# A transformer block on one core: fetches issued by ScalarE, row turns kept in order, masks ahead of the last additions, and three projections and splits moved

## The reference

```
h   = layernorm(x)                          # rows of 512
kqv = h @ Wqkv + bqkv                       # 16 heads of 32
s   = k q^T / sqrt(32); s = triu(s) - 10000 * tril(1, -1)
a   = softmax(s, axis=2) ; out = einsum('bnkq,bknh->bqnh', a, v)
x   = x + layernorm(out @ Wo + bo)
g,u = layernorm(x) @ Wg^T, layernorm(x) @ Wu^T   # Wg, Wu: 2048 x 512, (int - 128) * scale
x   = x + layernorm((silu(g) * u) @ Wd^T)   # the inner layernorm is of the new x
```

## Time and profile before

| What | Value |
|---|---|
| median of 3 runs | 1640.79 us (1640.74 to 1642.38) |
| profiled execution | 1639.89 us, of which span 1638.1 us |
| mean granted TensorE clock | 0.981 |
| TensorE busy | 1544.6 us, 94% of the span |
| VectorE, ScalarE, GpSimd busy | 57%, 49%, 36% |
| start, 0 to 78 us | TensorE busy 51.21 us, granted clock 0.91 |
| attention, 78 to 953 us | TensorE busy 816.92 us, granted clock 0.97 |
| feed-forward, 953 to 1638 us | TensorE busy 676.49 us, granted clock 1.00 |

### The profile page before, as it was taken

The page is one execution under the profiler, slowest core; times in us unless marked ns, Lnnn a source line. Parts: engine busy times, 40 slices in busy tenths (PEclk is TensorE's granted clock), DMA queues, the critical chain, the costliest instruction groups (busy, mean ns, idle before and its releaser), DMA issues.

```text
span 1638.1 us, 24488 instructions
## 1 busy us (share of the span) xinstructions
PE 1544.6 (94%) x9322; PEld 641.2 (39%) x9324; DVE 939.4 (57%) x1864; ACT 795.9 (49%) x1284; POOL 592.7 (36%) x809
## 2 busy tenths in 40 slices
PE   4899999998999999999977999999999999999997
PEld 2333334333333333333322244444444444444443
DVE  5666755788756887667756333564434343434344
ACT  5356676667666776667755633232222222222222
POOL 4335664677556766755755310020000000000001
PEclk8999999999999999999988999999999999999999
DMA  4212322224411233223345431221111111111000
GB/s 181 92 50 52 77 55 53 67 64 117 105 48 35 81 106 88 61 52 95 106 137 164 108 97 45 59 97 38 47 26 52 26 52 26 52 26 52 1 26 26
DMA packets 113398, 112.26 MB, mean 69 GB/s; under 512 B 69632, under 2 KB 69632, under 8 KB 113024
## 3 DMA queue, kind: packets, MB, share of 16 engines
q1 hardware_dynamic: 113280, 110.69, 23.7%
HBM read 45.37 MB, written 25.17 MB: 43 GB/s over the span
## 4 chain that ended last, share of the span: by engine, by line
PE 72%; DVE 10%; POOL 6%; ACT 4%; issue 4%; SPq 3%; DMA 1%; POOLq 0%; ACTq 0%; DVEq 0%
PE ps L976 25%; PE ps L897 16%; PE ps L993 12%; PE ps L960 10%; PE ps L934 5%; DVE mcol L1255 4%; SPq L753 3%; POOL pt L1467 2%; PE ps L910 2%; ACT pt L1109 1%; POOL rs L1387 1%; PE ps L918 1%; DVE st L1150 1%; DVE xh L650 1%; POOL pt L1458 1%
## 5 line engine op out<-in xcount | busy, mean ns | idle before, releaser
L1109 ACT ACTIVATE pt<-ps,nrm 128x512 f32<-128x512 f32 (+1 forms) x640 | 361.5, 647 | 222.0 <-PE ps L934 208.8
L976 PE MATMUL ps<-x2in,gu 128*128 128x512 f16 x2048 | 462.4, 379 | 0.1
L1255 DVE TENSOR_REDUCE mcol<-ps 128x1 f32<-128x512 f32 (+2 forms) x636 | 318.0, 566 | 139.3 <-PE ps L918 93.1
L976 PEld LDWEIGHTS ps<-x2in,gu 128*128 128x128 f16 x2048 | 200.2, 98 | 242.0 <-ACT sg L1130 0.6
L1384 POOL TENSOR_SCALAR rs<-mv 128x1 f32<-128x1 f32 x120 | 27.2, 226 | 652.4 <-DVE mv L1154 646.1
L1326 DVE SCALAR_TENSOR_TENSOR hf<-ps,usc,sg 128x512 f32<-128x512 f32 x128 | 96.1, 751 | 259.1 <-PE ps L976 245.6
L1135 ACT ACTIVATE hh<-hf 128x512 f16<-128x512 f32 x128 | 80.7, 631 | 258.8 <-DVE hf L1326 245.2
L1467 POOL TENSOR_TENSOR pt<-pt 128x1024 f32<-128x1024 f32 x84 | 201.5, 2421 | 1.8 <-ACT pt L1109 1.8
L934 PE MATMUL ps<-qpack,kpack 98*128 98x512 f16 (+3 forms) x768 | 163.6, 331 | 29.0 <-DVE mcol L1255 25.7
L993 PE MATMUL ps<-wd,hh 128*128 128x512 f16 x496 | 188.0, 379 | 0.0
L993 PE MATMUL ps<-wd,hl 128*128 128x512 f16 x496 | 188.0, 379 | 0.0
(11 more groups left out here) (125 smaller groups left out, 1592.8 us busy)
## 6 DMA issues: line engine op xcount, KB each, us to landing
qpack<-stage SPq DMA_DIRECT2D x192, 64.0 KB, 2.0
kpack<-stage SPq DMA_DIRECT2D x192, 64.0 KB, 2.0
xr<-in_x SPq DMA_DIRECT2D x32, 256.0 KB, 2.9
x1d<-xr SPq DMA_DIRECT2D x32, 256.0 KB, 2.3
x2d<-xh SPq DMA_DIRECT2D x32, 256.0 KB, 2.3
x1in<-x1d SPq DMA_DIRECT2D x8, 1024.0 KB, 5.8
out_x<-yy SPq DMA_DIRECT2D x32, 256.0 KB, 2.0
xin<-in_x SPq DMA_DIRECT2D x24, 256.0 KB, 2.9
```

The costliest lines, as they stand in the source:

```text
L976: mm = pe.matmul(bk, GU[:, c, m, i * 128:(i + 1) * 128], x2in[:, 1 - k, p, c, :], start=p == 0 and c == 0, stop=p == 1 and c == 3)
L1109: act.activation(Pt[:, PBUF[step], h, off:512], ps[:, BANK[job], off:512], ACT.Exp, scale=esc).then_inc(s_ex, 1)
L1255: mm = dve.tensor_reduce(mcol[:, n % 2, col:col + 1], scores, AX.X, ALU.max)
```

## The change

1. **Fetches by ScalarE.** A new job `act_fetch(i)` for i = 1 to 7 stands at the start of the step after the one that converts i - 1, and ScalarE issues the DMA. SP keeps fetches 0 and 8 to 23.
2. **Rows in order.** `row_work` keeps the normalised blocks in a list, and only the oldest of them may be turned. In steps 5 to 7 of the groups n % 4 == 1 nothing is turned.
3. **Projections.** In groups n % 4 == 2 the q and k projections stand at steps 3, 5, 7, 9 (before: 1, 3, 7, 9) and the v projections at 1, 2, 4, 6, 8 (before: 0, 2, 4, 6, 8). `qk(2, 0, 0)` leaves step (0, 1) and stands ahead of the groups, behind the last v projection and ahead of `packs(1)`.
4. **Sums.** In step 7 both additions stand behind the scores and masks (before: one ahead, one behind). The `den` of the summed blocks moves from step 9 to step 0 of the next group.
5. **Devs.** In steps 0 to 2 only the first `dev` stands ahead of the products; the others follow the scores.
6. **Halves of the result.** In groups 14 and 15 `halve` follows the scores.
7. **Split of Wo.** `split_o` 0 to 3 stand at (0, 3), (0, 4), (2, 3), (2, 4) (before: (0, 3) to (0, 6)).

```diff
--- before.py
+++ after.py
@@ -106,14 +106,15 @@
     b, g = divmod(n, 4)
     out = {}
     if n + 2 < NG:
-        for i, s in enumerate(((0, 2, 3, 7) if b else (1, 3, 7, 9), (0, 1, 2, 3), (1, 3, 7, 9), (1, 2, 3, 8))[g]):
-            out[s] = ("qk", n + 2, i % 2, i // 2)
+        for i, s in enumerate(((0, 2, 3, 7) if b else (None, 3, 7, 9), (0, 1, 2, 3), (3, 5, 7, 9), (1, 2, 3, 8))[g]):
+            if s is not None:
+                out[s] = ("qk", n + 2, i % 2, i // 2)
     if n == 0:
         for i, s in enumerate((0, 2, 5, 8)):
             out[s] = ("vproj", 4 + i)
     if b + 1 < B:
         first = 8 * b + 8 + (0, 0, 2, 7)[g]
-        for i, s in enumerate(((), (7, 9), (0, 2, 4, 6, 8), (0,))[g]):
+        for i, s in enumerate(((), (7, 9), (1, 2, 4, 6, 8), (0,))[g]):
             out[s] = ("vproj", first + i)
     if g == 3:
         for i, s in enumerate((5, 7, 9)):
@@ -147,7 +148,7 @@
         if g == 1 and b + 1 < B:
             chains += [(NS * n + (0, 1, 2, 3, 4, 5, 6, 7)[k], LN1, 8 * b + 8 + k) for k in range(8)]
     at = {}
-    untaken = 0
+    untaken = []
 
     def free(kind, step):
 
@@ -163,14 +164,19 @@
             kind = kinds[0]
             if kind == "residual" and ("wo_stats", t - 2) in at and at.get(("turn2", t - 2), step) >= step:
                 continue
-            if kind == "residual" and adding(step):
+            if adding(step) and (kind == "residual" or step // NS % 4 == 1 and kind in ("ln1_turn", "turn2")):
                 continue
             if kind == "ln1_stats" and t >= 10 and at.get(("ln1_norm", t - 2), step) + 2 > step:
                 continue
-            if kind in ("ln1_norm", "norm2") and untaken == 2 or kind in cost and not free(kind, step) and (
-                    room.get(step, 99) < cost[kind]):
+            if kind in ("ln1_norm", "norm2") and len(untaken) == 2 or (
+                    kind in ("ln1_turn", "turn2") and untaken[0] != t):
                 continue
-            untaken += {"ln1_norm": 1, "norm2": 1, "ln1_turn": -1, "turn2": -1}.get(kind, 0)
+            if kind in cost and not free(kind, step) and room.get(step, 99) < cost[kind]:
+                continue
+            if kind in ("ln1_norm", "norm2"):
+                untaken.append(t)
+            if kind in ("ln1_turn", "turn2"):
+                untaken.pop(0)
             if kind in cost and step in room and not free(kind, step):
                 room[step] -= cost[kind]
             at[kind, t] = step
@@ -186,13 +192,18 @@
     summed = step[0] < SUMS and step[1] == 1 and step[2] < 4
     out = [] if summed else [("den",) + step]
     out.append(("num",) + step)
-    if summed and step[2] > 0:
-        out += [("sum",) + step + (h,) for h in (0, 2) if h == 0 or s != 7]
-    return out + [("den", n, 1, 0)] * (s == NS - 1 and n < SUMS)
+    if summed and step[2] in (1, 2):
+        out += [("sum",) + step + (h,) for h in (0, 2)]
+    return [("den",) + step[:2] + (0,)] * (s == 0 and step[0] < SUMS) + out
 
 
 
 LAST = (124, 125, 126, 127)
+
+
+
+SPLIT_O = [(0, 3), (0, 4), (2, 3), (2, 4)]
+
 
 
 def order_of_jobs():
@@ -222,7 +233,7 @@
         if i == 6:
             plan += [("inverses", 3), ("vo_scale",)]
         add(("mjob", 0, i))
-    plan += [("mjoin", 0), ("mturn", 0)] + fill
+    plan += [("mjoin", 0), ("mturn", 0)] + fill + [("qk", 2, 0, 0)]
     plan += [("packs", 1), ("load_x", 8), ("load_x", 9)] + [("mjob", 1, i) for i in range(EARLY)]
 
     rows = {}
@@ -241,21 +252,27 @@
         for s, (j, kb) in enumerate(STEPS):
             here = rows.get(NS * n + s, [])
             add(("step", n, s))
-            plan += [("dev", DEV_FOR[job[0]], job[1]) for job in here if job[0] in DEV_FOR]
+            plan += [("act_fetch", i) for i in range(1, 8) if ffn_step(i - 1) + 1 == NS * n + s]
+            devs = [("dev", DEV_FOR[job[0]], job[1]) for job in here if job[0] in DEV_FOR]
+            soon = 1 if s < 3 else len(devs)
+            plan += devs[:soon]
             lot, of = (s + EARLY, n + 1) if s < NS - EARLY else (s + EARLY - NS, n + 2)
             if of < NG:
                 add(("mjob", of, lot))
             plan += [job for job in here if job[0] in ("ln1_turn", "turn2")]
-            if (s == 1 and n > 0) or s == 4:
-                add(("halve", n if s == 4 else n - 1, 0 if s == 4 else 1))
+            halve = [("halve", n if s == 4 else n - 1, 0 if s == 4 else 1)] if s == 4 or s == 1 and n > 0 else []
+            if n < NG - 2:
+                plan += halve
             products = products_of(pend, n, s)
             if n < NG - 2:
                 plan += products
-            plan += [("score", n, j, kb, h) for h in range(4)]
+            plan += [("score", n, j, kb, h) for h in range(4)] + devs[soon:]
+            if n >= NG - 2:
+                plan += halve
             if n < NG - 2 and pend is not None and last(*pend[1:]):
                 plan += [("invert",) + pend[:2], ("normalise",) + pend[:2]]
             if s == 7 and n < NG - 2:
-                add(("sum",) + pend + (2,))
+                plan += [("sum",) + pend + (h,) for h in (0, 2)]
             if s == NS - EARLY and n + 1 < NG:
                 plan += [("mjoin", n + 1), ("mturn", n + 1)]
             if n >= NG - 2:
@@ -263,8 +280,8 @@
                 if last(*pend[1:]):
                     plan += [("invert",) + pend[:2], ("normalise",) + pend[:2]]
             plan += [job for job in here if job[0] not in ("ln1_turn", "turn2")]
-            if n == 0 and s in (3, 4, 5, 6):
-                add(("split_o", s - 3))
+            if (n, s) in SPLIT_O:
+                add(("split_o", SPLIT_O.index((n, s))))
             if n == 0 and s in (7, 9):
                 add(("ffn_scales", s // 8))
             if s in ends:
@@ -274,7 +291,7 @@
             if n == NG - 3 and s == NS - 2:
                 plan += [("ffn_fetch", 10)]
             plan += [each for i in range(24) if ffn_step(i) == NS * n + s
-                     for each in [("ffn_load", i)] + [("ffn_fetch", k) for k in range(24) if RAW_BEFORE[k] == i]]
+                     for each in [("ffn_load", i)] + [("ffn_fetch", k) for k in range(8, 24) if RAW_BEFORE[k] == i]]
             pend = (n, j, kb)
         if n + 2 < NG:
             add(("packs", n + 2))
@@ -1108,6 +1125,11 @@
                     e.wait_ge(s_sc, NO[job])
                     act.activation(Pt[:, PBUF[step], h, off:512], ps[:, BANK[job], off:512], ACT.Exp, scale=esc
                                    ).then_inc(s_ex, 1)
+                elif kind == "act_fetch":
+                    i = a[0]
+                    e.wait_ge(s_cv["act"], i)
+                    ra, src, _ = raw_of_ffn(i)
+                    act.dma_start(ra, src).then_inc(d_raw[RAW[i]], 16)
                 elif kind == "ffn_load" and BY[a[0]] == "act":
                     i = a[0]
                     if FFN[i][0] == 4:
```

## The result

The changed kernel takes 1676.95 us (median of 4 runs, 1673.62 to 1678.29) against 1640.76 us before: ratio 1.0221, interval 1.0197 to 1.0245, so 36 us slower. The direction was forecast, the size was not: 1654.0 was predicted, and the range ended at 1664.

What follows compares the result with a forecast made beforehand. TensorE, busy for 94% of the span, was taken as the bound. Terms of 28.0 - 5.0 - 2.2 - 0.75 - 6.0 - 2.5 + 1.2 + 0.5 = +13.25 us gave 1654.0 us, range 1630 to 1664.

Steps and rivals of the forecast that it cites:

- Rows in order, +28: Groups 6 and 10: a transposition waits behind packs, TensorE comes late, then half clock; 14 us each, +28 (20 to 34).
- Masks ahead of the last additions, -0.75 and -2.2 in n = 13: Groups 4, 8, 12: 1.25 us mask waits go, devs take about 1 back, -0.75; group 13: 2.2 of 2.69 saved.
- The `den` only changes its step: Denominators of the summed blocks: moving them was taken to cost nothing.
- Devs: Groups 5, 9: freed rows save 3.5 us, step (5,2) loses most of its 2.00 wait, late devs cost 1.7; net -2.5 each.
- Fetches by ScalarE, -3.8: At n = 13: packs begin 2.6 us earlier, their first eight take 4.96 instead of 6.13; 3.8 us saved.
- the rival that was built on it: At n = 13: ScalarE's fetch saves only its issue, the pause stays at 9.60 us, time 1657; chance 8%.
- The remaining parts, +1.7 together: Start projection, split of Wo and moved projections in n = 0 and 2: +1.2; moved projections in n = 6, 10: +0.5.
- the split: Split of Wo: frees 0.85 us in n = 0 and costs about 0.5 in n = 2.
- the projections: Moved projections cost 0.25 us in each of n = 2, 6 and 10.
- Start: Projection ahead of group 0 lengthens the pause there by about 2.6 us; step (0,1) gives back 1.3.
- n = 1: Group 1: five waits make 3.0 us, turns leave their steps; -2.2 us (0 to -3).
- n = 15 with all behind it: Halves behind the scores in groups 14, 15: TensorE's 1.48 us wait and a later one go; -2.5 (-1 to -4.5).

Runs made afterwards that it cites:

- e3: Changed kernel, with the 24 DMAs of packs for groups 7 and 11 issued four a step in steps 0 to 5 of groups 6 and 10: 1650.39 us, ratio 1.0046.
- e5: Changed kernel, with VectorE's join of the maxima written as a one-operand reduction instead of a two-operand operation: 1669.16 us, ratio 1.0163.
- e1: Changed kernel, with the two last additions of step 7 placed as before: 1665.5 us, ratio 1.0141.
- e4: Kernel before, with one edit alone: both last additions of step 7 behind the scores and masks: 1649.41 us, ratio 1.0045.
- e2: Changed kernel, with the denominators of the summed blocks back in step 9: 1674.75 us, ratio 1.0194.
- e6: Changed kernel, with last additions and denominators placed as before and packs of groups 7 and 11 issued four DMAs a step: 1638.13 us, ratio 0.9975.
- e7: The kernel of e6, with all devs of steps 0 to 2 again ahead of the products: 1633.12 us, ratio 0.9945.
- e8: Kernel before, with one part of the change alone: fetches 1 to 7 issued by ScalarE: 1640.79 us, ratio 0.9998.
- e11: The kernel of e7, with all raw weights fetched by SP as before: 1635.09 us, ratio 0.9957.
- e12: The kernel of e11, with the projections of groups 2, 6, 10 and the split of Wo as before: 1628.76 us, ratio 0.9909.

## Why the prediction was right in direction and wrong in size

**Rows in order, +28: right.** The chain packs, transposition, ScalarE's half, exponentials, TensorE held link by link within 0.5 us, and taking it away gave 28.7 us (e3), 25.3 of them in groups 6 and 10 themselves.

**Masks ahead of the last additions, -0.75 and -2.2 in n = 13: the step that failed.** It looked at what stands behind the additions' old place (the masks) and not at what stands behind their new one. There is the join on VectorE, which is held while GpSimd adds (e5), and the exponentials of step 8, which wait for the additions. The two terms are 6 us of gain, less 3 us for the devs in n = 4, 8 and 12. In the place of the 6 us of gain the runs showed a loss of 13 us in the changed kernel (e1) and 7 us by itself (e4), or 8.9 and 10.5 us in groups 0 to 13 of the traces. How the loss divides between join, halves and exponentials is shown only for the join: written as a reduction it gave back 9.5 us (e5), which the intervals do not tell apart from the 13. The trace of before had the warnings: a VectorE half beside an addition at 2.61 us, which the prediction used, for the rows only, and joins of up to 1.42 us.

**"The `den` only changes its step", 0: wrong**, by a little: 0.5 us in each of the groups 3, 7 and 11 (e2), 0.6 with the additions back (e6 against e1), so 1.6 to 1.9 us; the 4 us of e2's median are not clear of the noise. Why it costs that was not tried by itself.

**Devs: right in sum.** The prediction's 2.5 for n = 5 and 9 comes out only as 3.5 + 0.7 - 1.7, so that 0.7 is what step (5,2) gains; its words can also be read as a gain of 1.3, and then the sum is 3.1. Late devs were so put at a net 1.0 each in n = 5 and 9, and at 1 in n = 4, 8, 12: 5 us. They cost about 5 us (e7): 0.8 and 0.9 in n = 4 and 8, 1.8 and 2.9 in n = 5 and 9, the rest spread. The rows without them gave 2.9 each in n = 5 and 9, not 3.5.

**Fetches by ScalarE, -3.8: the place right, the sum wrong.** SP's wait was won (2.8 us in the changed kernel, 3.7 in e8), but the transfer's own company and ScalarE's wait for its conversion were left out, and nothing is left in the time (e8; e11 does not tell it apart). The gain that the prediction added for the first eight packs was not there either: they took 4.98 us in the changed kernel, but all 24 together no less than before. The prediction set a rule of the Trainium skill against this part ("DMA: Bandwidth & Descriptors", section "Issuing engines are not separate DMA queues"). The trace agrees with its one half, that transfers started by different engines interleave: a row block of SP's beside a fetch of ScalarE's took 5.26 us. Its other half, that only the issue is saved, does not describe a queue whose head waits: SP's issue came 3.7 us earlier. As to the time, the rival that was built on it came nearer than the forecast, though the pause did shrink.

**The remaining parts, +1.7 together:** the split cost 1.8 net where -0.35 was put down; the projections, put at 0.75, cost between 0 and 4 us, part of it clock, and that stays open. **Start:** the pause and n = 0 cancel (predicted +1.3). **n = 1** gave -2.9 without late additions (predicted -2.2); **n = 15 with all behind it** took 2.4 to 2.8 us less in all runs with the moved halves (predicted -2.5).

The sum of errors: 15 to 19 us for the additions (9 to 13 lost where 6 were to be gained), 2 for the denominators, 6 for fetches and split make 23 to 27, near the 23 us between 1654 and 1677. The start alone, 2.8 us above its term in the trace, shows how far such a sum can be trusted.

## What to carry to other kernels

When a job is moved behind another in an in-order list, ask at the new place who shares a buffer, a port or a queue with it for as long as it lasts, not only who was freed at the old place. Here a run of 24 small DMAs was a wall of 16 us for whatever was issued behind it: put what somebody waits for ahead of it, or cut the run in pieces. And take a package of edits apart: here the rows in order were worth some 10 us (n = 1, 5, 6, 9 and 10 of e12 against before), hidden under the 29 us that the place of their DMAs cost and the 13 of another edit. And look at the clock of a group before its time is put down to an edit.

## What the runs showed of the hardware

- A VectorE operation of two SBUF operands on 16 columns took up to 2.31 us while GpSimd was adding; a reduction over the same numbers took 0.18 us in the same place of the list, beside the additions (e5).
- A 256 KB load that took 3.06 us from issue to its reader's start took 5.26 us with a 512 KB load issued 0.11 us behind it from another engine (e8); with 0.5 to 1.2 us between them it took 2.9 to 3.2 us.
- After 9.16 us of TensorE idle the clock was at 0.50 for the next 6.25 us, as after the 9.60 us of the kernel before.
- The same start of the program took 88.4 us with a granted clock of 0.98 from 35 us on (e1), and 93.0 us with 0.88 (the changed kernel).
